# Cross-attention on one Trainium2 core: turning the row maxima of a head pair on VectorE and moving the last two sums

## What is computed

```python
def _L0_xattn_ref(q, k, v):                 # q = layernorm(x), k = v = ctx_2048, each (4, 512, 512)
    b, d, m = q.shape; h = 8; c = v.shape[1]
    qh = q.reshape(b * h, d // h, m)        # 32 heads of 64 rows
    kh = k.reshape(b * h, d // h, -1)
    vh = v.reshape(b * h, c // h, -1)
    qk = jnp.einsum('bdm,bdn->bmn', qh, kh) / sqrt(64)
    sm = jax.nn.softmax(qk, axis=-1)
    return jnp.einsum('bmn,bcn->bcm', sm, vh).reshape(b, c, m)
x = x + attn(layernorm(x)); x = x + xattn(layernorm(x), ctx_2048); x = x + ffn(layernorm(x))
```

## Time and profile before

| | |
|---|---|
| median of 3 runs | 801.81 us (800.12 to 803.68) |
| the profiled execution's own time | 804.03 us |
| its span in the trace | 801.9 us |
| PE busy | 769.0 us, 96% |
| DVE busy | 639.2 us, 80% |
| ACT busy | 491.6 us, 61% |
| POOL busy | 423.4 us, 53% |

### The profile page before, as it was taken

The page is one execution under the profiler, slowest core; times in us unless marked ns, Lnnn a source line. Parts: engine busy times, 40 slices in busy tenths (PEclk is TensorE's granted clock), DMA queues, the critical chain, the costliest instruction groups (busy, mean ns, idle before and its releaser), DMA issues.

```text
span 801.9 us, 15448 instructions
## 1 busy us (share of the span) xinstructions
PE 769.0 (96%) x4902; PEld 423.2 (53%) x4902; DVE 639.2 (80%) x1905; ACT 491.6 (61%) x844; POOL 423.4 (53%) x458
## 2 busy tenths in 40 slices
PE   7999999999999999998998999999998899999997
PEld 6777544444444444444875555555543455555543
DVE  7676888889888888971689678888876798888883
ACT  4665467667767767765465455555556565576564
POOL 5554479999999600000334367777785344423321
PEclk9999999999999999999999899999999999999999
DMA  8898665445445212201485534444420011000001
GB/s 290 303 380 290 197 163 138 130 128 142 131 118 148 70 52 64 63 3 53 154 289 193 170 96 130 126 125 120 119 72 11 13 41 40 18 24 27 27 19 47
DMA packets 65760, 94.79 MB, mean 118 GB/s; under 512 B 26928, under 2 KB 38448, under 8 KB 64144
## 3 DMA queue, kind: packets, MB, share of 16 engines
q1 hardware_dynamic: 61216, 80.77, 31.8%
q0 software_dynamic: 3952, 12.98, 6.0%
q10 hardware_dynamic: 512, 0.07, 0.1%
HBM read 72.88 MB, written 20.51 MB: 116 GB/s over the span
## 4 chain that ended last, share of the span: by engine, by line
PE 32%; DVE 11%; issue 4%; ACT 2%; POOL 1%; DMA 1%; SPq 1%; ACTq 0%; DVEq 0%; POOLq 0%
PE r_p L1697 12%; PE r_p L1631 4%; PE r_pn L1644 4%; PE r_p L1727 3%; PE r_pn L1727 3%; DVE r_mx L1408 3%; DVE r_kl L1420 3%; PE r_p L1597 2%; PE r_p L1711 2%; DVE r_stats L1378 1%; DVE r_total L1438 1%; DVE tok L1397 1%; DVE r_inv L1445 1%; PE r_p L1579 1%; DVE r_xl L1391 1%
## 5 line engine op out<-in xcount | busy, mean ns | idle before, releaser
L787 ACT ACTIVATE b_probs<-ab_j 128x512 f32<-128x512 f32 (+1 forms) x352 | 177.1, 560 | 26.7 <-PE ab_j L852 15.8
L148 DVE CUSTOM_DVE_ANT_0 b_junk<-ab_t,mask_qk 128x128 bf16<-128x128 f32 (+2 forms) x243 | 108.8, 486 | 26.9 <-PE ab_t L128 26.8
L852 PE MATMUL ab_j<-qs,ks 98*128 98x512 bf16 (+1 forms) x352 | 123.3, 365 | 1.6 <-DVE a_rest L533 0.8
L1276 ACT ACTIVATE r_probs<-r_p 128x512 f32<-128x512 f32 x128 | 69.5, 599 | 72.3 <-PE r_p L1631 71.0
L148 DVE CUSTOM_DVE_ANT_0 b_junk<-ab_e,mask_qk 128x256 bf16<-128x256 f32 (+2 forms) x237 | 103.7, 482 | 1.8 <-PE ab_e L128 1.5
L1408 DVE TENSOR_REDUCE r_mx<-r_p 128x1 f32<-128x512 f32 x128 | 82.4, 675 | 23.9 <-PE r_p L1597 22.0
L1174 POOL TENSOR_TENSOR r_halves<-r_probs 128x1024 f32<-128x1024 f32 x32 | 77.3, 2414 | 38.5 <-DVE r_total L1438 26.9
L1323 ACT ACTIVATE r_silu<-r_p,r_cg 128x512 f32<-128x512 f32 x64 | 44.3, 692 | 51.4 <-PE r_p L1697 50.2
L870 PE MATMUL ab_pv<-b_probs,v 128*32 128x512 f32 (+3 forms) x1024 | 75.6, 436 | 0.0
L1201 POOL TENSOR_SCALAR r_h<-r_h,r_fh 128x1024 f32<-128x1024 f32 x32 | 37.9, 1198 | 64.1 <-DVE r_fh L1538 64.1
L128 PE MATMUL ab_e<-ks,qs 96*128 96x128 bf16 (+3 forms) x269 | 64.9, 304 | 4.1 <-DVE mx L148 0.9
(11 more groups left out here) (178 smaller groups left out, 1749.9 us busy)
## 6 DMA issues: line engine op xcount, KB each, us to landing
qs<-q_parts SPq DMA_DIRECT2D x32, 192.0 KB, 3.4
q_parts<-a_parts SPq DMA_DIRECT2D x15, 384.0 KB, 6.1
a_wst<-in_w_gate SPq DMA_DIRECT2D x4, 1024.0 KB, 7.5
a_wst<-in_w_up SPq DMA_DIRECT2D x4, 1024.0 KB, 9.9
a_wst<-in_w_down SPq DMA_DIRECT2D x4, 1024.0 KB, 8.4
qs<-q_parts SPq DMA_DIRECT2D x32, 128.0 KB, 3.3
b_wst<-in_w_gate POOLq DMA_DIRECT2D x16, 256.0 KB, 4.0
b_wst<-in_w_up POOLq DMA_DIRECT2D x16, 256.0 KB, 3.1
```

The lines of the kernel that those rows point to most:

```text
L148: best = nc.vector.tensor_tensor_reduce(out=junk[:, 2 * (st.use[i, k] % slots) + n, 0:w], in0=bank[:, c:c + w], in1=keep["mask_qk"][:, SEQ ...
L787: nc.scalar.activation(pblock(j % 2, kb)[:, j0:j0 + nj, c:c + w], p2[(NE * j + n) % BANKS2][:, 0:nj * w].rearrange("p (j c) -> p j c", j=n ...
L852: last = nc.tensor.matmul(bank, ks[0:STACK + 2, s, kb * P:(kb + 1) * P], qs[0:STACK + 2, s, j0:j0 + nj, kb * P + c:kb * P + c + w], start= ...
L1276: nc.scalar.activation(probs[:, 2 * (p % 2) + a, blk, :], p2_bank("s", j, n)[:], ACT.Exp, scale=SCALE).then_inc(p2_used, 1)
```

## The change

- `turn_maxima` moves from PE to DVE: one transpose of a pair's `mx`, now 32 columns wide (zero beyond the eight), within blocks of 32x32, into `mt`. T on PE, its turn at the `p1` banks and the negation on DVE go. `unit` holds -1 in place of 1.
- A block of 32 query rows now lies on partitions of its own in `mt`, so SP sends the maxima in four DMAs of 8 x 32 numbers in place of two of 4 x 128.
- PE waits for the rows ahead of the fourth term of S, not ahead of the first.
- The values `vt` of a pair come by one DMA of 256 KB in place of two of 128 KB. (The inverse sums are broadcast by two DMAs to 64 rows each, before and after.)
- `sum_probs(14)` stands behind W of the last pair. `sum_probs(15)` and ACT's copy of it move from body 38 into feed 4, behind its third `gate_up` and third `gate`.

PE in an even body in the middle of the cross-attention, before. Names: `r_mrows,r_unit` is the fourth term of S, `r_total,ones` the sum, `r_probs,r_vt` W, `ident,r_mx` is T and `r_kh,r_qh` of L1597 is F.

The diff:

```diff
--- before.py
+++ after.py
@@ -919,7 +919,7 @@
         mrows = m.sb("mrows", [P, 2, DIM], F32R); unit = m.sb("unit", [P, P], F32R)
         vt = m.sb("vt", [P, UNROLL, KD, H])
         halves = m.sb("halves", [P, 2, DIM]); total = m.sb("total", [P, UNROLL, DIM])
-        mx = m.sb("mx", [P, 2, 2 * KD]); mrow = m.sb("mrow", [2 * KD, 2, P], F32R)
+        mx = m.sb("mx", [P, 2, H // 2]); mt = m.sb("mt", [P, 2, H // 2])
         den = m.sb("den", [P, DIM]); few = m.sb("few", [2 * RUNS, 2, H]); inv = m.sb("inv", [2 * RUNS, 2, H])
         rden = m.sb("rden", [P, DIM]); y = m.sb("y", [P, UNROLL, DIM])
 
@@ -954,6 +954,7 @@
         kh_done, kl_done = m.sem("kh_done"), m.sem("kl_done")
         p1_full, p1_used = m.sem("p1_full"), m.sem("p1_used")
         scores, p2_used, halved, summed, weighted = (m.sem(s) for s in ("scores", "p2_used", "halved", "summed", "weighted"))
+        mt_done = m.sem("mt_done")
         first_total, second_total = m.sem("first_total"), m.sem("second_total")
         few_in, inv_done, inv_out, rden_in = (m.sem(s) for s in ("few_in", "inv_done", "inv_out", "rden_in"))
         y_kept, y_done, x2_done = m.sem("y_kept"), m.sem("y_done"), m.sem("x2_done")
@@ -996,15 +997,13 @@
             for n in range(STEP):
                 if 0 <= i - 1 < HEADS_X:
                     p1_use["f", i, n] = len(p1_use)
-            if i >= 2 and i % 2 == 0 and (i - 2) // 2 < PAIRS:
-                p1_use["turn", (i - 2) // 2] = len(p1_use)
             for n in range(STEP):
                 if 0 <= i - 4 < HEADS_X:
                     p2_use["s", i - 4, n] = len(p2_use)
             if i >= 8 and i % 2 == 0 and (i - 8) // 2 < PAIRS:
                 p2_use["sum", (i - 8) // 2] = len(p2_use)
         P1_USES, P2_USES = len(p1_use), p2_use["s", HEADS_X - 1, STEP - 1] + 1
-        LATE_SUMS = PAIRS - 2
+        LATE_SUMS, LAST_SUM_BODY = PAIRS - 2, E_FIRST + 2
 
         def p1_bank(*key):
             return p1[p1_use[key] % BANKS]
@@ -1034,13 +1033,15 @@
                 sp.dma_start(ql[:, p % LSLOTS, :].bitcast(F32), scr["xl"][P * p:P * (p + 1), :]).then_inc(ql_in[p % LSLOTS], 16)
 
             def load_maxima(p):
-                sp.wait_ge(p1_used, p1_use["turn", p] + 1)
+                sp.wait_ge(mt_done, p + 1)
                 if p == 0:
                     sp.wait_ge(padded, 2)
                 if due(STEP * 2 * (p - 1)):
                     sp.wait_ge(scores, STEP * 2 * (p - 1))
-                for a in range(2):
-                    sp.dma_start(mrows[a * H:a * H + 1, p % 2, :].bitcast(F32), mrow[a * KD:(a + 1) * KD, p % 2, :].bitcast(F32)).then_inc(m_in[p % 2], 16)
+                rows = mrows[0:H + 1:H, p % 2, :].bitcast(F32).rearrange("a (k g c) -> a k g c", k=KD, g=KD)
+                for g in range(KD):
+                    at = g * P // KD
+                    sp.dma_start(rows[:, :, g, :], mt[at:at + 2 * KD, p % 2, :]).then_inc(m_in[p % 2], 16)
 
             def attend_output(i):
                 for j in range(2) if i == 0 else (i + 1,):
@@ -1088,9 +1089,8 @@
                 if p is not None:
                     if due(p - 1):
                         sp.wait_ge(weighted, p - 1)
-                    for a in range(2):
-                        sp.dma_start(vt[:, 2 * (p % 2) + a, :, :], io["ctx_t"][bass.ds(2 * p + a, 1)].rearrange("o (k p) c -> p (o k) c", p=P)
-                                     ).then_inc(vt_in[p % 2], 16)
+                    sp.dma_start(vt[:, 2 * (p % 2):2 * (p % 2) + 2, :, :], io["ctx_t"][bass.ds(2 * p, 2)].rearrange("o (k p) c -> p o k c", p=P)
+                                 ).then_inc(vt_in[p % 2], 16)
                 p = pair_due(i, 11)
                 if p is not None:
                     sp.wait_ge(inv_done, p + 1)
@@ -1128,10 +1128,11 @@
         @block.gpsimd
         def _(pool):
             nc.gpsimd.memset(mrows[:].bitcast(F32), 0.0)
+            nc.gpsimd.memset(mx[:], 0.0)
             nc.gpsimd.memset(unit[:].bitcast(F32), 0.0).then_inc(padded, 1)
             pool.wait_ge(padded, 1)
-            nc.gpsimd.memset(unit[0:1, :].bitcast(F32), 1.0)
-            nc.gpsimd.memset(unit[H:H + 1, :].bitcast(F32), 1.0).then_inc(padded, 1)
+            nc.gpsimd.memset(unit[0:1, :].bitcast(F32), -1.0)
+            nc.gpsimd.memset(unit[H:H + 1, :].bitcast(F32), -1.0).then_inc(padded, 1)
             pool.wait_ge(padded, 2)
 
             def deviation(sems, i):
@@ -1294,11 +1295,14 @@
                 exponential(2)
                 exponential(3)
                 p = pair_due(i, 8)
-                if p is not None:
-                    act.wait_ge(summed, p + 1)
-                    if due(p):
-                        act.wait_ge(few_in, 32 * p)
-                    nc.scalar.activation(den[:], p2_bank("sum", p)[:], ACT.Copy).then_inc(p2_used, 1)
+                if p is not None and p < PAIRS - 1:
+                    keep_sums(p)
+
+            def keep_sums(p):
+                act.wait_ge(summed, p + 1)
+                if due(p):
+                    act.wait_ge(few_in, 32 * p)
+                nc.scalar.activation(den[:], p2_bank("sum", p)[:], ACT.Copy).then_inc(p2_used, 1)
 
             def quantised(j):
                 if not 0 <= j < TILES:
@@ -1347,6 +1351,8 @@
                 quantised_products(1)
                 keep_turned_products(0)
                 gate(2)
+                if i == LAST_SUM_BODY:
+                    keep_sums(PAIRS - 1)
                 quantised(i - 1)
                 keep_turned_products(1)
                 gate(3)
@@ -1404,14 +1410,16 @@
                 if not 0 <= i - 1 < HEADS_X:
                     return
                 p, a, blk = unit_of(i - 1, n)
+                if p1_use["f", i, n] == 0:
+                    dve.wait_ge(padded, 1)
                 dve.wait_ge(p1_full, p1_use["f", i, n] + 1)
                 nc.vector.reduce_max(mx[:, p % 2, KD * a + blk:KD * a + blk + 1], p1_bank("f", i, n)[:], AX.X).then_inc(p1_used, 1)
 
-            def keep_maxima(p):
-                dve.wait_ge(p1_full, p1_use["turn", p] + 1)
+            def turn_maxima(p):
+                dve.wait_ge(p1_used, STEP * 2 * (p + 1))
                 if p >= 2:
-                    dve.wait_ge(m_in[p % 2], 32 * (p // 2))
-                nc.vector.tensor_scalar(mrow[:, p % 2, :], p1_bank("turn", p)[0:2 * KD, 0:P], -1.0, None, ALU.mult).then_inc(p1_used, 1)
+                    dve.wait_ge(m_in[p % 2], 64 * (p // 2))
+                nc.vector.transpose(mt[:, p % 2, :], mx[:, p % 2, :]).then_inc(mt_done, 1)
 
             def keys_low(p):
                 dve.wait_ge(kh_done, p + 1)
@@ -1426,7 +1434,7 @@
                 if c in KEYS_LOW_AT:
                     keys_low(KEYS_LOW_AT[c])
                 if c == TURN_AT:
-                    keep_maxima(0)
+                    turn_maxima(0)
 
             def attend_context(i):
                 maximum(i, 0)
@@ -1449,7 +1457,7 @@
                     keys_low(p)
                 maximum(i, 3)
                 if p is not None and p >= 1:
-                    keep_maxima(p)
+                    turn_maxima(p)
                 p = pair_due(i, 13)
                 if p is not None:
                     dve.wait_ge(rden_in, 32 * (p + 1))
@@ -1597,16 +1605,9 @@
                     nc.tensor.matmul(p1_bank("f", i, n)[:], qh[rows, p % QSLOTS, blk * P:(blk + 1) * P], kh[rows, p % UNROLL, :],
                                      start=True, stop=True).then_inc(p1_full, 1)
 
-            def turn_maxima(p):
-                use = p1_use["turn", p]
-                pe.wait_ge(p1_used, use)
-                nc.tensor.transpose(p1_bank("turn", p)[0:2 * KD, 0:P], mx[:, p % 2, :], keep["ident"][:]).then_inc(p1_full, 1)
-
             def early(c):
                 if c in BLOCKS_AT:
                     first_scores(*BLOCKS_AT[c])
-                if c == TURN_AT:
-                    turn_maxima(0)
 
             def second_scores(j, b):
 
@@ -1619,13 +1620,14 @@
                         pe.wait_ge(C["x1"], TILES - 1)
                     pe.wait_ge(kl_done, p + 1)
                     pe.wait_ge(ql_in[p % LSLOTS], 16 * (p // LSLOTS + 1))
-                    pe.wait_ge(m_in[p % 2], 32 * (p // 2 + 1))
                 for term, (left, right) in enumerate(((kh[:, p % UNROLL, :], qh[:, p % QSLOTS, :]), (kl[:, p % 2, :], qh[:, p % QSLOTS, :]),
                                                       (kh[:, p % UNROLL, :], ql[:, p % LSLOTS, :]), (unit, mrows[:, p % 2, :]))):
                     for a in range(2):
                         use = p2_use["s", j, 2 * b + a]
                         if term == 0 and due(use - SBANKS + 1):
                             pe.wait_ge(p2_used, use - SBANKS + 1)
+                        if term == 3 and a == 0 and b == 0 and j % 2 == 0:
+                            pe.wait_ge(m_in[p % 2], 64 * (p // 2 + 1))
                         rows = slice(a * H, (a + 1) * H)
                         weights = unit[rows, :] if term == 3 else left[rows, blk * P:(blk + 1) * P]
```

(11 more changed lines are left out.)

## The result

The changed kernel takes 790.82 us (median of 4 runs, 788.98 to 792.21), against 802.37 us of before on the same chip: a ratio of 0.9855, with a 95% interval of 0.9834 to 0.9876, or 11.6 us less (10.0 to 13.3). 7.9 us less was forecast. Run again unchanged in another set it takes 789.11 us (788.45 to 791.43, 4 runs) against 801.77, ratio 0.9842 (0.9821 to 0.9862). So it is faster, by more than was forecast.

A forecast was written before the change was run, and what follows sets the result against it. PE was taken to bound the loop (busy 10.15 of 10.26 us a pair). Terms -5.4 + 0 + 0 - 0.1 - 2.4 = -7.9 us gave 793.9 us from the median of 801.81, range 790.8 to 799.0 us.

The forecast's parts named there:

- the entry: Start of the cross-attention loop: pair 1's transpose leaving PE gives 0.8 us; pair 0's was given nothing.
- Part 1: Cross-attention loop on PE: the transpose leaves, 0.33 us in each of 14 pairs, 4.6 us; with pair 1, -5.4 us.
- Part 2: DVE in the loop: the transpose takes 0.25 us, covered by the wait and negation it replaces; 0 us.
- Part 3: SP's queue: four DMAs for the rows land 0.5 us before the fourth term of S needs them; 0 us.
- rival of the rows as the bound: S of each new pair: rows 0.95 us late in 14 pairs, +13.3 us, giving 807.2 us; chance 0.06.
- Part 4: Seam behind the loop: sum of pair 14 behind W covers PE's 0.84 us wait, but `silu` starts later; -0.1 us.
- Part 5: Feed 4: sum of pair 15 placed there removes PE's 2.54 us wait; -2.4 us.
- all of it counts: Rival: the whole 0.84 us at pair 14's sum and a little PE idle in the last bodies count; 792.3 us, chance 0.08.
- the pair of 9.92 us: Sign in the profile after: a pair of the cross-attention loop takes 9.92 us, against 10.26 before.
- the wait for `hq`: Sign in feed 3: PE's wait there grows by the 0.7 us handed on by moving the sum of pair 14.
- the others: Remaining signs: no PE idle ahead of F, DVE waiting only for F, transpose under 0.4 us, last sum without idle.

The follow-up runs named there:

- turn_kept: The changed kernel with PE's transpose of the maxima and its bank turn kept, result unused, DVE's transpose waiting for it: 796.79 us, ratio 0.9941 to before.
- wait_first: The changed kernel with PE's wait for the rows back ahead of the first term of S: 791.56 us, ratio 0.9868 to before.
- before_again: The kernel before, unchanged, run and profiled again: 802.41 us, ratio 1.0005 to before.
- eight_pieces: The changed kernel with each of the four DMAs of the rows cut in two: 806.49 us, ratio 1.0062 to before.
- before_cleared: The kernel before, with POOL clearing mx at the part's start and DVE waiting for it: 801.77 us, ratio 0.9997 to before.
- entry_filled: The changed kernel with 8 unread matmuls in PE's first wait at the cross-attention's entry and 4 in feed 3: 790.62 us, ratio 0.9856 to before.
- values_twice: The changed kernel with a pair's values loaded by two DMAs again, as before: 789.54 us, ratio 0.9837 to before.
- both_small: The changed kernel with the unread matmuls of entry_filled and the two value DMAs of values_twice: 790.72 us, ratio 0.9853 to before.
- after_again: The changed kernel, unchanged, run and profiled again: 789.11 us, ratio 0.9842 to before.
- before_filled: The kernel before, with unread matmuls in PE's waits, 3 ahead of the sum of pair 14 and 10 ahead of pair 15's: 800.12 us, ratio 0.9968.
- turns_only: The changed kernel with both last sums and ACT's copy of the last one back in their old places: 799.00 us, ratio 0.9946 to before.
- late_15_only: The changed kernel with the sum of pair 14 back in its old place: 794.43 us, ratio 0.9895 to before.
- one_weigh: The changed kernel with a pair's four blocks of W in one group in the even body: 799.49 us, ratio 0.9969 to before.
- late_14_only: The changed kernel with the sum of pair 15 and ACT's copy of it back in their old places: 793.04 us, ratio 0.9869 to before.

## Why the prediction was wrong, step by step

The mechanism of each part held; what failed are sizes. Of the 2.8 us that the stages show beyond the 7.9 forecast, 1.2 (0.7 by the most cautious pair of profiles) are the entry, which I sized by T alone, without the wait for the rows; 0.9 are T in the loop, 0.33 us a pair in place of 0.39; 0.6 are the sum of pair 14. What the medians show beyond the stages is not explained by any part, and its cause stays open.

**Part 1, the turns in the loop (forecast -4.6 for 14 pairs): -5.4.** The mechanism holds: with T kept, the whole gain is gone (`turn_kept`). The term was 0.33 us a pair and measures 0.39. I took W ahead of T as 1.87 us, from a W between an odd body's S and F. In the even body W stands behind the sum and takes 510.21 - 508.39 = 1.82 us, so T cost 516.69 - 514.49 - 1.82 = 0.38 us.

**The entry (forecast -0.8): -2.0.** This is the step with the largest error. I counted only T of pair 1. The wait for the rows stood ahead of the first term and moved to the fourth, and I had priced that move in the loop alone, where it is worth 0.1 us. At the first pair PE stands in it: 0.9 to 1.4 us by `wait_first`. The turns of the first two pairs are 0.7 us there (11.97 us in `turn_kept` against 11.27), close to what I had.

**Part 2, the transpose (0): right.** The transpose takes 0.18 to 0.21 us, and DVE still idles some 1.3 us a pair for the first scores.

**Part 3, four DMAs (0): right, and with more room than I gave it.** An issue takes 0.56 us where I took 0.65, and, the larger error, I took the landing from the old two-row form. Behind the end of its last issue that form's wait ends after 2.0 us at the entry (before and `before_again`), that of the four pieces after 1.1 (`wait_first`), that of the eight after 1.0. The rival of the rows as the bound is real, but begins between four and eight pieces. The rule of the Trainium skill (DMA: Bandwidth & Descriptors, "Specifications") that a transfer needs 512 B for the line rate would make the pieces land later than the old form; the trace shows them landing sooner. `eight_pieces`, with pieces of half the size, is slow by its 4.75 us of issues and what they push back in SP's queue.

**Part 4, sum 14 (forecast -0.1): -0.6 to -0.7.** Two sizes were wrong. I had the sum start at 605.46, which is 13.99 us behind the 29th W group; it starts 13.69 behind it, so the copy comes at 14.8 us (13.9 before) and `silu`, which had waited 0.79 us for PE, starts 0.07 us later and not 0.4. And `silu`'s start is not what carries on to `hq`. DVE's second product (of `silu` and the `up` matmuls) waited for PE before, and PE's second `up` now comes 0.89 us earlier (17.25 us behind the group, 18.14 before). That product before (19.27 us behind the group) and after (18.73), where it waits no more:

```profile
610.74 0.69 DVE L1492 TENSOR_TENSOR r_h<-r_p,r_silu 128x512 f32<-128x512 f32 x1 [0.32 <-PE r_p L1697]
```

```profile
600.89 0.68 DVE L1500 TENSOR_TENSOR r_h<-r_p,r_silu 128x512 f32<-128x512 f32 x1
```

These 0.54 us go through to `hq`. I had named this path and took 0.1 us of it.

**Part 5, sum 15 (forecast -2.4): -2.5.** Right.

**The sum.** -7.9 was forecast, and the rival nearest to what came (*all of it counts*, 792.3 us) looked for the rest in the seam; the stages give -1.98 - 5.49 - 0.68 - 2.52 = -10.7 (-10.6 from end to end). The measured 11.6 and 12.7 us of the two sets are 1 to 2 us more. Of 81 executions of before, `before_again` and `before_cleared`, 38 ran at a mean clock of 0.991; of 25 of the changed kernel and its near versions (`wait_first`, `entry_filled`, `values_twice`, `both_small` and `after_again`) one did, so before has more half clock. Where it lies isn't shown. `before_filled` suggests that the idles at its sums bring a part of it, and `turns_only` shows that such idles can, but no profile of before has half clock there. Another place fits as well: before's executions at 0.991 take 802.79 us on average, 2.5 more than those at 0.998, and 2.5 us is what 6.8 us of half clock cost at the start of the part (59.27 against 56.75 us), in code that the change doesn't touch.

Moving the sums is worth more together with part 1 than alone: 5.1 us on before (4.5 by the ratio), 8.2 us on `turns_only` (7.3 by the ratio). By the stages it is 3.0 and 6.9 us; of the 3.9 between them 0.7 is the loop's gain that the first `total` would have taken back, and the rest the half clock of that profile.

Of my own tells, the pair of 9.92 us came out at 9.83 and the wait for `hq` at 1.22 us instead of 0.89, 0.3 us longer where I expected 0.7; the others came as written. That PE shows no wait for the rows at the first pair either, I had not foreseen.

## What to carry to other kernels

When a wait is moved behind work that doesn't need it, price it at every place where it binds, the first round above all, and not only in the steady loop. A wait of PE behind a faster loop gets longer, since the producer hasn't become faster, and it may cost the clock of what follows as well. A queue that issues DMAs for several purposes is priced as a whole: what is put into it early delays what waits in it later. Before pricing by a stage, look where the profiled execution's half-clock stretches lie, and compare stages of executions that have them in the same places.

## What the runs showed of the hardware that I had not expected

- PE's granted clock fell to half for 3.4 us at idles of 1.55 us (`turns_only`), 1.62 us (`late_15_only`), 2.54 us (`turns_only`) and 2.74 us (`one_weigh`), and not at one of 2.53 us (`late_14_only`). No profile with the sums of before had it there, with idles of 0.83 to 0.86 and 2.54 us. A stretch of 3.4 us cost little at the entry (11.27 us with it, 11.30 without), where PE waits for DVE anyway, and 1.7 us at the first sum (30.39 us from the 29th W group to `hq` against 28.72 filled). At 376 us one of 3.4 us costs 1.6 us and one of 6.8 us 2.5 us (58.3 and 59.25 against 56.75).
- With 3 and 10 matmuls of 512 columns that nobody reads in these two waits the profile has no half clock there, and the kernel was 3.4 us faster by the ratios (4.6 by the medians) than without them.
- A transpose of 128x32 on DVE within blocks of 32 took 0.18 to 0.21 us. A DMA issue of 1 KB on SP took 0.56 us, and one of half that size 0.59 us. The wait for the rows at the entry ended 1.1 us behind the last issue for four pieces on eight partitions each, and 2.0 us behind it for the two DMAs of before; why is not shown.
